# Twelve search digits of a router moved into the attention loop, its counting given to GpSimd

## The reference, cut to what matters

```python
capacity = max(1, int(Sz * CAP_FACTOR / E) + 1)          # 257 of 1024 tokens
scores = jax.nn.softmax(jnp.einsum('bsd,ed->bse', x, router_w), axis=-1)
scores_t = jnp.swapaxes(scores, 1, 2)
gate_vals, sel_idx = jax.lax.top_k(scores_t, capacity)
```

## Time and profile before

| | us |
|---|---|
| Median of three executions | 1969.65 |
| Lowest and highest | 1968.38, 1974.62 |
| The profiled execution, its own time | 1974.67 |
| Its span, first to last instruction | 1972.9 |
| TensorE busy in it | 1739.6 |
| VectorE busy | 1400.5 |
| ScalarE busy | 1148.6 |
| GpSimd busy | 582.7 |

### The profile page before, as it was taken

One profiled execution on the slowest core, in us unless ns is written; L12 is line 12 of the kernel. 1 busy time (PEld: TensorE's weight loads), 2 busy tenths in 40 slices (PEclk: granted clock), 3 DMA queues, 4 the chain that ended last, 5 costly groups with the idle time before them and its releaser, 6 DMA issues. The chain is left out here.

```text
span 1972.9 us, 40754 instructions
## 1 busy us (share of the span) xinstructions
PE 1739.6 (88%) x15061; PEld 898.0 (46%) x15061; DVE 1400.5 (71%) x3172; ACT 1148.6 (58%) x2314; POOL 582.7 (30%) x817
## 2 busy tenths in 40 slices
PE   5699999999999968799659999999999999587895
PEld 2356666666666545576322222222222332155663
DVE  6576776667788455533569999999899998656431
ACT  3436666666656633222337998999888888332231
POOL 2312222121122146677440000002400000157774
PEclk9779999999999978988778999999999999589888
DMA  4642744553541044232230000000000000062324
GB/s 152 171 81 51 130 93 75 101 96 64 102 83 18 23 124 82 33 61 37 63 138 7 32 20 18 19 33 19 18 18 21 29 4 23 17 172 38 61 39 84
DMA packets 108005, 120.95 MB, mean 61 GB/s; under 512 B 14360, under 2 KB 72960, under 8 KB 107808
## 3 DMA queue, kind: packets, MB, share of 16 engines
q1 hardware_dynamic: 83616, 100.97, 21.7%
q0 software_dynamic: 24192, 17.38, 6.5%
HBM read 81.71 MB, written 35.65 MB: 59 GB/s over the span
## 5 line engine op out<-in xcount | busy, mean ns | idle before, releaser
L1252 DVE TENSOR_REDUCE mx<-wide 128x2 f32<-128x1024 f32 x512 | 593.4, 1217 | 37.5 <-PE wide L1154 35.4
L1286 ACT ACTIVATE pT<-bank 128x512 f32<-128x512 f32 x1024 | 556.7, 596 | 84.2 <-PE bank L1147 73.4
L903 ACT ACTIVATE pT<-bank 128x512 f32<-128x512 f32 (+3 forms) x768 | 344.2, 490 | 239.7 <-PE bank L757 230.3
L1154 PE MATMUL wide<-k_st,q_st 48*128 48x512 bf16 x1024 | 324.3, 400 | 23.7 <-DVE mx L1252 13.9
L1147 PE MATMUL bank<-q_st,k_st 51*128 51x512 bf16 x1024 | 329.9, 394 | 13.6 <-ACT pT L1286 2.5
L1163 PE MATMUL bank<-pT,vst 128*32 128x256 f32 x4096 | 336.6, 402 | 0.0
L870 DVE TENSOR_REDUCE mx<-wide 128x1 f32<-128x640 f32 (+3 forms) x256 | 256.7, 1021 | 91.0 <-PE wide L772 86.9
L757 PE MATMUL bank<-q_st,k_st 122*128 122x512 f32 (+3 forms) x768 | 297.5, 397 | 7.0 <-ACT pT L903 5.0
L764 PE MATMUL wide<-k_st,q_st 120*128 120x512 f32 (+3 forms) x768 | 271.8, 371 | 20.6 <-PEq L371 12.1
L1871 POOL DMA_INDIRECT acc_rows<-yg,idx x128 | 202.1, 1579 | 101.7 <-DVE yg L2138 66.0
L1147 PEld LDWEIGHTS bank<-q_st,k_st 51*128 51x128 bf16 x1024 | 73.7, 94 | 252.9 <-ACT pT L1286 198.1
(11 more groups left out here) (328 smaller groups left out, 2003.7 us busy)
## 6 DMA issues: line engine op xcount, KB each, us to landing
q_st<-rope_split SPq DMA_DIRECT2D x60, 256.0 KB
k_st<-rope_split SPq DMA_DIRECT2D x60, 256.0 KB
qk_split<-parts SPq DMA_DIRECT2D x8, 1024.0 KB, 6.5
q_st<-qk_split SPq DMA_DIRECT2D x96, 64.0 KB
k_st<-qk_split SPq DMA_DIRECT2D x96, 64.0 KB
qk_parts<-parts SPq DMA_DIRECT2D x8, 768.0 KB, 4.6
xn_rows<-xn SPq DMA_DIRECT2D x8, 512.0 KB, 3.9
w1b<-in_L_ffn_w SPq DMA_DIRECT2D x16, 256.0 KB, 5.0
```

The costliest lines, as they stand in the source:

```text
L903: e.activation(pT[:, u % NPB, q0:HALF], bank[place_of[u]][:, q0:HALF], ACT.Exp, scale=scale).then_inc(s_p, 1)
L1154: e.matmul(wide[w % 2][:, r * HALF:(r + 1) * HALF], q_st[at][64 * r:64 * r + MROW, pair, q0:q0 + P], k_st[at][64 * r:64 * r + MROW, pair, ...
L1252: e.tensor_reduce(mx[G % 2][:, kh, pair:GH:2, c], wide[w % 2][:, :].rearrange("p (r k) -> p r k", r=2), AX.X, ALU.max).then_inc(s_sf, 1)
L1286: e.activation(pT[:, u % NPB, :], bank[place_of[u]][:, :], ACT.Exp, scale=scale).then_inc(s_p, 1)
```

## The change

- The four steps of logits and the softmax move to slots 11 and 14 of five successive halves, 19 to 23, each with the bank that is idle in that half (`idle_bank`). The empty first two steps stay at half 18 without a lent bank. GpSimd's two normalizing multiplications (`pool_norm`) move 10 slots earlier.
- Twelve of the 15 digits move into halves 24 to 29, two in each half. The first is tried on VectorE at the end of slot 3, counted on GpSimd at its slot 3, summed on TensorE at the end of slot 8 (16 columns of the idle bank, reserved for two slots), and read on VectorE at the start of slot 9. The second has slots 10, 15 and 16.
- For these twelve the count is made by GpSimd (`pool_digits`): three comparisons of 128x128, one chain of seven additions that halve the width, and the matmul of TensorE as before.
- GpSimd's split of the maximum is listed at slot 7 in place of slot 11, which puts it between the two digits.
- The last three digits and the steps after them keep their form and begin at slot 487.

```diff
-            LENT = range(9, 15)
-            step_at = [2 * NP * s + at for s in LENT for at in (11, 14)]
-            last_of = [2 * NP * s + 14 for s in LENT]
+            LENT, COUNTED = range(19, 24), range(24, 30)
+            idle_bank = lambda h: 2 + (h + 1) % 2
+            digits = [(NP * h, first) for h in COUNTED for first in (True, False)]
+            digit_tried = {begin + (3 if first else 10): i for i, (begin, first) in enumerate(digits)}
+            digit_summed = {begin + (8 if first else 15): i for i, (begin, first) in enumerate(digits)}
+            digit_read = {begin + (9 if first else 16): i for i, (begin, first) in enumerate(digits)}
+            step_at = [18 * NP + at for at in (11, 14)] + [NP * h + at for h in LENT for at in (11, 14)]
...
-                uses += [(2 * NP * s + 14, 2 * NP * s + 19, 3, ("lent", s)) for s in LENT]
+                uses += [(NP * h + 14, NP * h + 19, idle_bank(h), ("lent", h)) for h in LENT]
+                uses += [(t, t + 2, idle_bank(t // NP), ("digit", i)) for t, i in digit_summed.items()]
...
                         if t - 3 in step_at:
-                            s = (t - 3) // (2 * NP)
-                            e.wait_ge(s_y, PRIME + 2 * s)
-                            e.wait_ge(s_m, PRIME + 2 * s + 2)
...
+                        if t in digit_summed:
+                            bank_free(ahead_of["digit", digit_summed[t]])
+                            next(steps)
...
+                        if t in digit_read:
+                            next(steps)
+                            e.sem_inc(s_lent, 1)
...
+                        if t in digit_tried:
+                            next(steps)
...
-                        if t in (19 * NP + 10, 19 * NP + 12):
+                        if t in (19 * NP, 19 * NP + 2):
                             next(normed)
...
-                        G = turns_max(t)
+                        G = turns_max(t + 4)
...
+                        if t in digit_tried:
+                            next(counted)
...
+            def pool_digits(self, e):
...
+                for i in range(len(self.sums)):
+                    e.wait_ge(self.inv, i + 2)
+                    for j in range(3):
+                        ins = e.tensor_scalar(hits[:, j, :], self.byrow[:, :], self.trials[:, j:j + 1].bitcast(F32), None, ALU.is_ge)
+                    then(ins)
+                    width = P // 2
+                    while width > 1:
+                        then(e.tensor_tensor(hits[:, :, 0:width], hits[:, :, 0:width], hits[:, :, width:2 * width], ALU.add))
+                        width //= 2
+                    if i:
+                        e.wait_ge(self.tot, PRIME + i)
+                    e.tensor_tensor(self.count[:, :], hits[:, :, 0], hits[:, :, 1], ALU.add).then_inc(self.cnt, 1)
+                    yield
...
+                    if i < len(self.sums):
+                        if i == 0:
+                            then(e.tensor_copy(self.trials[:, :], digit_units[:, 0, :]))
+                        else:
+                            then(e.scalar_tensor_tensor(self.trials[:, :], digit_units[:, i, :], self.taken[:, 0:1],
+                                                        self.found[:, :].broadcast_to([P, 3]), ALU.bitwise_xor, ALU.bitwise_xor))
+                            mark(e.tensor_tensor(self.found[:, :], self.found[:, :], self.taken[:, :], ALU.bitwise_xor))
+                        e.sem_inc(self.inv, 1)
```

More of the change, by code:

```diff
@@ L1139, in bank_free @@
                             e.wait_ge(s_m, PRIME + n + 1)
+                        elif kind == "digit":
+                            e.wait_ge(s_lent, len(LENT) + n + 1)
                         else:
@@ L1481, in mk_program, with __init__ @@
             STEPS, EARLY = 30, 12
-            def __init__(self, buf, h, side, counts, kept, late=None):
+            def __init__(self, buf, h, side, counts, kept, late=None, sides=None, sums=()):
                 self.h, self.side, self.by_pool = h, side, late is not None
+                self.sides, self.sums = sides or [side] * 5, sums
+                self.hits = buf("hits", [P, 3, P]) if sums else None
                 by_pool, self.late = self.by_pool, late[0] if late else side
-                self.gp, self.inv = (sem("pool_chain", False), sem("inverse", False)) if by_pool else (None, None)
+                self.gp, self.inv = (sem("pool_chain", False), sem("inverse_trials", False)) if by_pool else (None, None)
+                self.chained = 0
                 self.square = buf("square", [P, NC, D]) if by_pool else None
@@ L1508, in __init__, with logits, total_of @@
                 self.known = sem("gates_known")
-                self.logits = counts[:, 0:CPH * NE].rearrange("p (c e) -> p c e", c=CPH)
+                self.counts = [one[:, HALF - 2 * CPH * NE:HALF] for one in sides] if sides else [counts] * 4
                 self.totals = (late[1] if late else counts)[:, CPH * NE:CPH * NE + 16]
+            def logits(self, q):
+                return self.counts[q][:, 0:CPH * NE].rearrange("p (c e) -> p c e", c=CPH)
+            def total_of(self, i):
+                return self.sums[i] if i < len(self.sums) else self.totals[:, 0:3]
             def xn_of(self, q, c):
@@ L1542, in pool_sums @@
             def pool_sums(self, e):
-                n, parts = [0], self.lnv[:, :, :]
+                parts = self.lnv[:, :, :]
                 x = x_sb[:, self.h * 2 * NC:(self.h + 1) * 2 * NC, :]
@@ L1639, in vector @@
                 e.wait_ge(self.t, PRIME + 1)
-                then(e.tensor_copy(self.byrow[:, :], self.side[:, 0:P]))
+                then(e.tensor_copy(self.byrow[:, :], self.sides[4][:, 0:P]))
                 yield
@@ L1713, in scalar @@
                     e.wait_ge(self.tr, PRIME + q + 1)
-                    e.activation(self.xnT[q % 2][:, :], self.side[:, :], ACT.Copy).then_inc(self.ev, 1)
+                    e.activation(self.xnT[q % 2][:, :], self.sides[q][:, :], ACT.Copy).then_inc(self.ev, 1)
                     yield
@@ L1728, in tensor @@
                     for c in range(CPH):
-                        ins = e.transpose(self.side[:, c * P:(c + 1) * P], self.xn_of(q, c), ident[:, :])
+                        ins = e.transpose(self.sides[q][:, c * P:(c + 1) * P], self.xn_of(q, c), ident[:, :])
                     ins.then_inc(self.tr, 1)
@@ L1738, in tensor @@
                 e.wait_ge(self.pr, PRIME + 1)
-                e.transpose(self.side[:, 0:P], self.prob.rearrange("p c b e -> p (c b e)"), ident[:, :]).then_inc(self.t, 1)
+                e.transpose(self.sides[4][:, 0:P], self.prob.rearrange("p c b e -> p (c b e)"), ident[:, :]).then_inc(self.t, 1)
                 yield
@@ L1742, in tensor @@
                     e.wait_ge(self.cnt, PRIME + i + 1)
-                    e.matmul(self.totals[:, 0:3], same_row[:, :], self.count[:, :], start=True, stop=True).then_inc(self.tot, 1)
+                    e.matmul(self.total_of(i), same_row[:, :], self.count[:, :], start=True, stop=True).then_inc(self.tot, 1)
                     yield
```

31 lines of the change are left out of this document (19 added, 12 removed).

## The result

The changed kernel takes 1967.52 us, median of 20 executions (1963.16 to 1977.15), against 1972.54 us of the kernel before, also 20 (1967.87 to 1980.56). The ratio is 0.9972, 95% interval 0.996 to 0.9983: 5 us or 0.28% faster. Forecast were 1968 and -1.7 us, with a range of 1961 to 1979.

What follows compares the result with a forecast made beforehand. TensorE and VectorE were both taken to be at their limit in the loop, with a low clock at the end. Loop +7.3 and end -9.0 gave -1.7 us from the 1969.65 median: 1968, range 1961 to 1979.

Steps and rivals of the forecast that it cites:

- The loop, forecast +7.3: Main loop: 1.3 us a half, 7.8 us for six digit halves (4.5 to 13.0), less 0.5 for the lent bank.
- the lent banks should give -0.5: Half 18: the sixth, empty lent bank goes, six slots at 0.12 us less; the five used ones keep their price.
- 1.10 us a half from VectorE: Digit halves: reads of 0.42 and trials of 0.39 us; slot 3's trial goes into idle time, the rest is paid.
- 0.2 for banks and matmuls: Digit halves on TensorE: 0.84 us for lost banks plus two small matmuls, mostly covered, 0.2 us a half charged.
- GpSimd not waited for: Loop: counts ready before TensorE asks, first with 1.2 us or more to spare, second 0.5 to 1.0 us.
- my 3.6 and my bound of 4.1: GpSimd in the loop: time in us for the count of one digit, and its upper bound.
- The end, forecast -9: Behind slot 487: last turning 11.9 us earlier if the clock stays at 2.4 GHz, less 2.8 for a fall.
- The two waits of 1.55 and 1.6 us: Behind slot 487: TensorE waits for VectorE's chain up to slots and gates, then up to the last sum.
- my 8: Behind slot 487: some 8 us at the lower clock level, losing 2.8 us.
- The 1.0 us a slot by ScalarE: Slots behind 495 at full clock: ScalarE's two exponentials of 0.5 us each set the slot.
- The clock that stays down to the end: Rival: clock falls at slot 493 and stays down, end gains 0.9 us, whole +6.4, 1976 us; chance 0.25.
- Late counts: Rival: GpSimd's counts come late in the loop, 1975 to 1990, said 1978 us; chance 0.14 together with a dearer loop.

Runs made afterwards that it cites:

- Steps alone: All 15 digits behind slot 487, logits moved as in the changed kernel, copies of a digit's small VectorE steps in halves 24 to 29: halves of 20.51 to 20.58 us, first 20.90.
- the banks alone: Logits moved, all 15 digits behind slot 487, idle bank reserved at slots 8 and 15 of halves 24 to 29 without a digit: 20.47 us a half.
- the experiment with the longer count: Changed kernel with two more unread comparisons ahead of each GpSimd count, 1.2 us more a digit: 21.72 us a half.
- the logits alone: Changed kernel's logits in five successive halves, but all 15 digits behind slot 487 on VectorE as before: ratio to before 0.999.
- the counts on VectorE: Changed kernel with the twelve loop digits counted on VectorE, not GpSimd: 22.05 us a half, first to last join 641.21 us.
- the late steps spread: Changed kernel with TensorE's last six router steps at slots 487, 489, 491, 493, 497 and 502: ratio to before 0.9948.
- six digits twice: Two kernels, one digit a half in 24 to 29, nine behind the loop: own bank, ratio to before 0.9914; summed at slot 11 in the turned maximum's bank, 0.9936.
- fifteen late twice: Two profiles of one kernel: logits moved, all 15 digits behind slot 487, no step listed at slot 500; ratio to before 0.9979.

## Why the prediction was right, step by step

**Direction, place and mechanism held; the closeness of the number is luck.** The loop pays and the end gives more back. But the medians moved by -5.0 us where -1.7 was forecast, three times as much: the loop was 2.3 us cheaper than its term, the end gained 1.0 us more, and both misses went the same way. That 1968 lies half a microsecond from 1967.52 comes from the other side: the forecast stood on the median of three executions, 1969.65, and that of twenty is 1972.54.

**The loop, forecast +7.3, measured +5.0.** Of the miss 1.0 us is no term of the sum: the first halves of the trace of before ran slow for that long, ahead of the change. From the third join on the loop pays 591.77 - 585.81 = 6.0 us. The six digit halves give 6.2 of 7.8 forecast, the rest is -0.2, where the lent banks should give -0.5; a short fall of the clock in each of the two traces, some 1 us each, lies in these halves, so the -0.5 is neither shown nor refuted.

**The digit's steps, 1.10 us a half from VectorE and 0.2 for banks and matmuls.** This is the term that was mis-sized, 1.3 for a measured 0.96. Steps alone cost 0.96, the banks alone 0.87, both 0.96. A read was dearer than I took it (from one maximum to the next 0.49 us over the plain distance, not 0.42), and a trial about as dear (1573.00 - 1572.63 = 0.37 us, not 0.39), but VectorE had more to absorb them with than the one idle row of 0.52 us shows; and of the banks nothing came on top, where I had charged 0.2.

**GpSimd not waited for: right, and closer than I said.** A count took 4.43 us, above both my 3.6 and my bound of 4.1. A comparison lasted about 0.6 us, where the nearest rows gave 0.3 to 0.46. The second digit had 0.4 us to spare, not 0.5 to 1.0, and the experiment with the longer count bears the 0.4 out. The rule of the Trainium skill (GPSIMD Engine Reference, section 3.1) points the way of that miss: 0.60 us against VectorE's 0.34 for a comparison over 128x128 is 1.8 times, near the factor of 1.96 that it gives for an addition of two tensors. It decides nothing here, since counting on VectorE was 9 us dearer in the loop.

**The end, forecast -9, measured -10.0.** The two waits of 1.55 and 1.6 us were 1.09 and 1.42. The clock fell and came back, 6.8 us of it against my 8. The 1.0 us a slot by ScalarE was exact. One reading was off: in the trace of before the clock didn't fall behind the wait of 1.80 us but inside it, 1.0 us from its start.

```profile
1678.50:1679.50 1.00, 0.00 (x0) 0.00 (x0) 0.89 (x6) 0.60 (x1) 0.00 (x0) 1.00 0.00 0
1679.53:1680.30 0.77, 0.00 (x0) 0.00 (x1) 0.77 (x7) 0.00 (x0) 0.00 (x0) 0.50 0.00 0
```

The forecast of a fall doesn't hang on that. Its 8 us were taken from one fall in the loop, and there luck had a part: behind the loop the clock stayed down for 3.4 to 44.4 us in the profiles here.

**The rivals.** The clock that stays down to the end didn't come with this kernel, in two profiles; the nearest to it are the 17.1 us with the same listing behind slot 487. I had held against it that router steps with waits in two slots of three are what keeps the clock down. The profile of VectorE's steps alone speaks against that. Its 15 digits stand behind slot 487 as before, TensorE waited 1.80 us up to 1664.23, and then its stretches are:

```profile
1664.30:1666.30 2.00, 2.00 (x20) 0.62 (x20) 1.50 (x11) 1.24 (x3) 0.00 (x0) 1.00 0.00 0
1666.40:1673.20 6.80, 6.80 (x42) 1.62 (x42) 3.76 (x27) 4.04 (x8) 0.00 (x0) 0.50 0.01 2
1673.30:1683.40 10.10, 7.27 (x74) 2.27 (x66) 8.12 (x45) 7.12 (x14) 0.00 (x0) 1.00 0.00 0
```

The clock came back after 6.8 us with two more digits summed in them, at 1668.88 and 1672.10. So what decides how long it stays down is open. Late counts didn't come, and the experiment with the longer count shows that they were 0.4 us away.

**What I didn't see** is where the 48 us of before came from. I named the one wait and the fall of the clock, but took the stretch for the price of 15 digits all the same. The kernel with all 15 behind the loop and no step at slot 500 reaches its last turning in 35.6 us and the next layer in 44.27, 8.6 less than before. So in the traces most of what the change gained at the end was the one wait behind the turned output and the time at the lower clock that went with it, and a list of slots would have bought that without the loop paying 6 us. In the medians that kernel isn't shown to be faster than the changed one, 0.9979 against 0.9972.

## What to carry to other kernels

Before moving work away from a stretch, look for the wait that makes the stretch slow: here an in-order engine had a digit listed behind an output that came later, and the clock fell in that wait. Where two engines are both at their limit, a charge to each can lie side by side with the other and not on top, as 0.87 and 0.96 us made 0.96 here; measure each alone before adding them. A slow engine is the right place for work exactly while nobody waits for it, and what is queued behind that work on the same engine decides as much as its length.

## What the runs showed of the hardware

Three profiles have a wait of TensorE of 1.8 us behind slot 487 at a granted clock of 2.4 GHz. It fell to 1.2 GHz 1.0 and 1.1 us into the wait in two (before, the logits alone) and 2.2 us behind its end in the third (VectorE's steps alone). In three with waits of 1.09 and 1.42 us, 3 us apart (the changed kernel twice, the counts on VectorE), it fell 0.7 to 0.8 us into the second. In the five in which neither was listed (the late steps spread, six digits twice, fifteen late twice) it stayed at 2.4 GHz up to the last turning, with TensorE busy for 30.05 of 32.60 us in the first of them.

Such waits aren't needed for a fall. Eleven profiles have two small waits ahead of the first two late sums, of 0.8 or 1.07 us and of 0.43 us. In four of them the clock fell there, for 3.4, 10.2, 17.1 and 44.4 us, in seven it didn't, and nothing here shows what parts the four from the seven. How long the clock stayed down after the longer waits varied too: 6.8 us in four profiles, 27.3 us in two.

The Trainium skill (TensorE: Matmul & The Clock Gate, Part 1) has it that activity releases the slow state; the returns after 6.8 us agree. That TensorE's rows touch is no sign of it: they did for 24.92 of 26 us in the kernel of the logits alone, and the clock stayed down.

A GpSimd comparison of 128x128 f32 with a scalar from a tile took 0.60 us, a halving addition over 192 columns and five more behind it 2.31 us.
